# A state-space and mixture-of-experts layer on one core: the last scan direction and the last batch by token halves

## The chip, the core and the metric

The kernel runs on one core of a Trainium2 chip. The core has five instruction queues that run side by side and in order, each by itself: PE (TensorE, matrix products and transposes), DVE (VectorE), ACT (ScalarE), POOL (GpSimd) and SP (SyncE, which only issues transfers here). They wait for one another through semaphores. The metric is the device time of one execution in microseconds; less is better.

## The reference, cut to what matters

The input x has 8 batches of 1024 tokens and 256 features, all in float32. A batch goes through two blocks, each `x + layernorm(block(layernorm(x)))`.

```python
def _mamba_block(x, ...):                  # ED = 512 channels, N = 16 states
    xz = x @ W_in.T
    y = _ssm_branch(xf, zf, ...)           # tokens in order
    y_b = _ssm_branch(xb, zb, ...)         # tokens reversed, other weights
    return ((y + y_b[:, ::-1, :]) * 0.5) @ W_out.T

def _ssm_branch(...):
    x = silu(causal_depthwise_conv(xz_half)); delta = softplus(...)
    # for each token: h = exp(delta * A) * h + delta * B * x ;  y = sum over the states of h * C
    return (y + Dp * x) * silu(z)

def _L0_ffn_ref(hidden, ...):              # 8 experts, the best 2 of each token, and a shared one
    ...
```

The second block sends each token to its two best experts of eight (256 to 512 to 256) and adds a shared expert that all tokens go through.

## The kernel before, in words

**Scans.** A batch has two directions, so there are 16 windows w; the odd ones scan the tokens backwards. In a window there are 16 states n times 4 channel blocks c of 128 channels: 64 units, 1024 in all. Unit k needs on ACT one exponential, `feed_decay` (decay, 128 x 1024, in PSUM, two buffers), on POOL one product, `feed_drive` (xu times a row of B broadcast over the partitions, three buffers), and on DVE one `tensor_tensor_scan` over 1024 tokens, `scan_unit`. After the four units of a state the result h is turned to token-major by PE in 8 tiles of 128 tokens (`turn_tile`), and each tile is multiplied by its column of C and added to y (128 x 512): by DVE for three tiles of four (`sum_tile`), by ACT and POOL for the fourth (`scale_tile`, `pool_tile`; tiles 2, 6, 10 and 14 of 16). The rows of B come by `b_row_load`, one of 1024 tokens for each state, into two buffers. SP issues it as soon as the four drives of the state two before are made.

**Everything else is side work**, written out by hand as a list of pieces in `side_work`: the tokens' norm, the input projection (`proj`), the four taps of the convolution (`tap0` on ACT, `tap` on DVE), delta (`dt_mm`, `softplus`, `delta`), `u_mul` on POOL that turns xu into delta times x, and for a batch whose two windows are done the mixing: `y_dump` and `y_load` of y through DRAM, `z_mm`, `y_turn`, `y_add`, `gate`, `out_mm`, then norm, residual and norm (`ln_stats`, `ln_var`, `ln_rstd`, `ln_apply`, `res_add`), `xn2_turn`, the router, the routing on DVE (`peak`, `top1`, `top2`, `slots`; `owner_hot` is its last result), the `scatter` of the tokens to their experts' blocks by indirect DMA, the shared expert (`h1_mm`, `gelu`, `eo_mm`), the routed experts in six groups of four blocks (`xs_load`, `xs_turn`, `r1_mm`, `rgelu`, `r2_mm`, `ys_store`), the `gather` of their results, and the combine (`comb_mm`, `comb`), the last norm, `fin_add` and `out_store`.

**The order.** Time is cut into slots. Scan unit k stands in slot 2k on DVE, its drive in slot 2k-4 on POOL, its decay in slot 2k-3 on ACT; tile i is turned in slot i+7 and added in slot i+8 (POOL's in i+9). The table `AT` gives each piece of side work a due time, and `due // 16` is its slot (`Plan.put`). An engine goes through the slots and issues what stands in each. So `AT` fixes the order on each engine, and the semaphores fix the time. `BANK_USE` orders the uses of two PSUM banks by the side work in the same way. Window w starts at slot 128 w; the last, w = 15, at 1920, and the last scan stands in slot 2046. From b = 2 on, the batches in the middle have the same places, 256 slots apart.

**The end.** Batch 6's experts run beside window 15; its `gather` stands in slots 2061 to 2071. Batch 7 is mixed whole after that: first `y_turn` in slot 2087, last `out_mm` in 2117, `slots` in 2143, the first `xs_turn` in 2171, the first `gather` in 2262, the last `fin_add` in 2282.

`DMA_RING_BYTES` is given to the program as the size of the scratch for the descriptors that POOL makes for its indirect DMAs.

## Time and profile before

| | |
|---|---|
| median of 3 runs (lowest, highest) | 4735.8 us (4734.28, 4736.21) |
| the profiled execution | 4736.2 us |
| its span | 4735.0 us, 52683 instructions |
| PE busy | 3366.6 us (71%) |
| DVE busy | 3978.3 us (84%) |
| ACT busy | 2975.1 us (63%) |
| POOL busy | 3570.4 us (75%) |
| scan, L1104 | 1024 x 2.278 us |
| drive, L1567 | 1024 x 2.361 us |
| moved by DMA | 687.42 MB, 145 GB/s |

A line of a view names the line of the kernel, the engine, the operation and the tiles. "Idle before" is the time for which the engine stood still just before an instruction, with the releaser, the work that ended last among what it waited for; "issue" is idle time in which the profile shows nothing that it waited for. The execution's time is 1.2 us more than its span; that part lies outside what the trace shows.

### The profile page before, as it was taken

The page shows a single profiled execution, that of the slowest core. Times are in us where ns is not written, and L with a number is a line of the kernel's source. Part 1 is how long each engine was busy: PE and PEld are TensorE (multiplying, and loading weights), DVE is VectorE, ACT ScalarE, POOL GpSimd, SP SyncE. Part 2 cuts the span into 40 slices and gives each one's busy share as a digit, 9 for nine tenths or more (in the row PEclk, how much of TensorE's full clock was granted, in tenths as well). Part 3 has the DMA queues.
Part 4 walks back from the last instruction along what each step waited for, and adds up shares of the span by engine and source line. Part 5 has one row for each costly group of instructions (what it writes and reads, how often), then busy time and mean ns, then how long its engine had stood idle before and what let it go on. Part 6 is the DMA issues. An engine that isn't in the chain of part 4 may idle for free.

```text
span 4735.0 us, 52683 instructions
## 1 busy us (share of the span) xinstructions
PE 3366.6 (71%) x16720; PEld 2441.2 (52%) x16720; DVE 3978.3 (84%) x4136; ACT 2975.1 (63%) x4196; POOL 3570.4 (75%) x2119
## 2 busy tenths in 40 slices
PE   3466767786678857787778867777677866787575
PEld 1344445564456645565446644566446554476354
DVE  2899999898989989898989989898898989898200
ACT  4455756686657856686657856577566866576343
POOL 2698877978878878878879778887879788797111
PEclk8566777998779968898879977899779987798787
DMA  4321332555335642466325553356325553255244
GB/s 120 117 82 64 114 106 95 174 191 181 126 102 186 214 151 93 142 202 206 125 76 194 193 169 125 114 188 224 133 83 165 189 196 134 98 184 175 66 161 149
DMA packets 362017, 687.42 MB, mean 145 GB/s; under 512 B 31874, under 2 KB 205451, under 8 KB 357643
## 3 DMA queue, kind: packets, MB, share of 16 engines
q1 hardware_dynamic: 349450, 650.48, 41.5%
q0 software_dynamic: 12288, 33.57, 2.2%
q8 instruction: 133, 2.18, 0.2%
q14 instruction: 146, 1.19, 0.1%
HBM read 513.04 MB, written 170.92 MB: 144 GB/s over the span
## 4 chain that ended last, share of the span: by engine, by line
DVE 36%; POOL 21%; issue 21%; ACT 9%; PE 8%; DMA 4%; SPq 0%; DVEq 0%; POOLq 0%; ACTq 0%
DVE h L1104 17%; POOL drive L1567 12%; DVE y L1119 10%; DVE side L1182 3%; POOL y L1575 3%; POOL xs_dram L1620 2%; POOL work L1631 2%; ACT decay L1311 2%; DVE stats L1163 1%; POOL xu L1589 1%; PE h_t L947 1%; PE side L1082 1%; ACT work L1525 1%; ACT scaled L1329 1%; ACT work L1519 1%
## 5 line engine op out<-in xcount | busy, mean ns | idle before, releaser
L1567 POOL TENSOR_TENSOR drive<-xu,b_row 128x1024 f32<-128x1024 f32 x1024 | 2408.4, 2361 | 354.1 <-DVE h L1104 350.6
L1104 DVE TENSOR_TENSOR_SCAN h<-decay,drive 128x1024 f32<-128x1024 f32 x1024 | 2332.4, 2278 | 148.1 <-POOL drive L1567 121.7
L947 PE MATMUL h_t<-ident,h 128*128 128x128 f32 x8192 | 1472.0, 318 | 852.2 <-DVE y L1119 544.6
L947 PEld LDWEIGHTS h_t<-ident,h 128*128 128x128 f32 x8192 | 1092.6, 162 | 1355.9 <-DVE y L1119 807.3
L1311 ACT ACTIVATE decay<-delta,neg_a 128x1024 f32<-128x1024 f32 x1024 | 1142.7, 1117 | 874.5 <-DVE h L1104 841.2
L1119 DVE SCALAR_TENSOR_TENSOR y<-h_t,c_col,y 128x512 f32<-128x512 f32 x1488 | 1065.1, 732 | 65.6 <-PE h_t L947 64.1
L1575 POOL TENSOR_TENSOR y<-y,scaled 128x512 f32<-128x512 f32 x496 | 630.6, 1271 | 185.6 <-ACT scaled L1329 182.9
L1082 PE MATMUL side<-expert_w,work 128*128 128x256 f32 x1472 | 400.8, 424 | 69.1 <-issue 34.6
L1074 PE MATMUL side<-xn_t,expert_w 128*128 128x128 f32 x2944 | 388.5, 277 | 38.9 <-DVE xu L1182 14.8
L1329 ACT ACTIVATE scaled<-h_t,c_col 128x512 f32<-128x512 f32 x496 | 340.4, 686 | 115.0 <-PE h_t L947 113.8
L1074 PEld LDWEIGHTS side<-xn_t,expert_w 128*128 128x128 f32 x2944 | 355.0, 192 | 50.7 <-DVE xu L1182 17.7
L1082 PEld LDWEIGHTS side<-expert_w,work 128*128 128x128 f32 x1472 | 300.2, 213 | 128.1 <-issue 44.0
L1631 POOL DMA_INDIRECT work<-ys_dram,slot_i x128 | 123.6, 966 | 245.6 <-DMA ys_dram<-work 215.0
L1589 POOL TENSOR_TENSOR xu<-xu,prep_work 128x1024 f32<-128x1024 f32 x64 | 150.8, 2357 | 150.7 <-DVE prep_work L1149 150.7
L1182 DVE SCALAR_TENSOR_TENSOR side<-prep_work,chan_sb,side 128x512 f32<-128x512 f32 x256 | 191.9, 750 | 78.9 <-ACT side L1358 74.3
L1281 DVE TENSOR_TENSOR acc<-side,acc 128x512 f32<-128x512 f32 x32 | 21.7, 677 | 252.5 <-PE side L1059 244.1
L1519 ACT ACTIVATE work<-side,b_blocks 128x128 f32<-128x128 f32 x736 | 207.4, 365 | 40.2 <-PE side L1074 40.2
L1620 POOL DMA_INDIRECT xs_dram<-work,slot_i x128 | 126.3, 987 | 114.3 <-DVE owner_hot L1275 68.6
L985 PE MATMUL side<-dbc,wdt_sb 97*128 97x512 f32 x256 | 161.2, 734 | 13.2 <-DVE prep_work L1149 5.9
L965 PE MATMUL side<-xn_t,w_in_sb 128*128 128x512 f32 x256 | 136.4, 662 | 40.8 <-DVE xu L1182 30.4
L1059 PE MATMUL side<-work 128*128 128x256 f32 x256 | 104.8, 551 | 70.6 <-DMA work<-ys_dram,slot_i 54.1
L1003 PE MATMUL side<-w_out_sb,work 128*128 128x256 f32 x512 | 137.4, 419 | 21.8 <-POOL work L1611 14.5
(148 smaller groups left out, 3735.7 us busy)
## 6 DMA issues: line engine op xcount, KB each, us to landing
expert_w<-in_w SPq DMA_DIRECT2D x384, 512.0 KB, 4.2
b_row<-b_dram SPq DMA_DIRECT2D x256, 512.0 KB, 4.1
dx_dram<-prep_work SPq DMA_DIRECT2D x64, 512.0 KB, 3.7
delta_dram<-prep_work SPq DMA_DIRECT2D x64, 512.0 KB
delta<-delta_dram SPq DMA_DIRECT2D x64, 512.0 KB, 4.2
work<-xs_dram SPq DMA_DIRECT2D x40, 512.0 KB, 4.0
ys_dram<-work SPq DMA_DIRECT2D x40, 512.0 KB, 6.0
xz_dram<-prep_work SPq DMA_DIRECT2D x32, 512.0 KB, 2.7
```

Of the source, the lines that this page charges most:

```text
L947: t = pe.e.transpose(h_t[i % N_H_T][:, c * P:(c + 1) * P], h[:, gn % 2, c, tb * P:(tb + 1) * P], ident[:, :])
L1074: mm = pe.e.matmul(bank[:, m * P:(m + 1) * P], wi[:, k, m * P:(m + 1) * P], xn2_t[:, k, at:at + P], start=(k == 0), stop=(k == DC - 1))
L1082: mm = pe.e.matmul(bank[:, q % 2 * D:(q % 2 + 1) * D], h1_blocks[:, q, m, :], wo[:, m, :], start=(m == 0), stop=(m == HC - 1))
L1104: dve.e.tensor_tensor_scan(o, a, v, 0.0, ALU.mult, ALU.add).then_inc(scanned, 1)
L1119: dve.e.scalar_tensor_tensor(out=y[:, tb, :], in0=h_t[i % N_H_T][:, :], scalar=c_n, in1=y[:, tb, :], op0=ALU.mult, op1=ALU.add).then_inc(s ...
L1182: op = dve.e.scalar_tensor_tensor(out=into, in0=xz_pad[:, at:at + BANK], scalar=chan_col(d, c, CHAN_CONV_W + k), in1=bank[:, :], op0=ALU.m ...
L1311: act.e.activation(decay[k % N_DECAY][:, :], delta[:, c, :], ACT.Exp, scale=neg_a[:, c, w % 2, n:n + 1]).then_inc(decay_made, 1)
L1329: act.e.mul(into, h_t[i % N_H_T][:, :], c_col[:, w % 2, tb, n:n + 1]).then_inc(tile_scaled, 1)
L1519: op = act.e.activation(h1_blocks[:, q, m, :], side[bank_of["r1_mm", index]][:, m * P:(m + 1) * P], ACT.Identity, bias=b1_blocks[:, m, j:j ...
L1567: pool.e.tensor_tensor(drive[:, k % N_DRIVE, :], xu[:, w % 2, c, :], b_row[:, gn % N_B_ROW, :], ALU.mult).then_inc(drive_made, 1)
L1575: pool.e.tensor_tensor(y[:, tb, :], y[:, tb, :], scaled[:, at % N_SCALED, :], ALU.add).then_inc(gathered, 1)
L1620: pool.e.indirect_dma_start(out=xs_dram, out_offset=bass.IndirectOffsetOnAxis(ap=slot_i[:, r, tb:tb + 1], axis=0), in_=tokens[:, tb, :], i ...
```

## The change

1. The last window (`SPLIT` = 15) is scanned by halves of 512 tokens: first tokens 512 to 1023 for all 16 states, then tokens 0 to 511. A unit is now two channel blocks times 512 tokens, so there are still 64 units; each has two scans and two exponentials and one drive product of the same size. The state at the border is kept by ACT (`keep_h`, 16 copies of 128 x 4) and is the start of the second half's scans. The rows of B are loaded by halves: 32 loads of 512 tokens in the place of 16 of 1024. Tiles go to engines by the same rule.
2. The last batch is mixed by halves. Its first half is the one that the scan finishes first. Its `z_mm` and `z_silu` are done for both halves in window 15 (slots 1923 to 1993), `y_turn` to `out_mm` for the first half in 2004 to 2034, with the first norm's statistics and the residual up to 2043. y is turned from where it lies: `y_dump` and `y_load` fall away for this batch. z, the tokens and one of two buffers of the experts' inner results are put where `xu` of the even window lay, the sums in `prep_work`, the shared expert's inner result in a part of y. Norm, residual, norm, `x1_store`, the last norm and `out_store` are by halves.
3. For all batches: the bias product of `eo_mm` moves to `comb_mm`; `diag` moves from `work` to `xn2_t` (so `xn2_copy` waits for the combine of the batch before); x1 has two places in DRAM; `xn2_turn` and `xn2_copy` go by token half first, and `h1_mm` waits for its half alone; `top1` waits for the `mix_turn` of the batch before.
4. `DMA_RING_BYTES` is 2048 in the place of 1024.
5. All places in `AT` and `BANK_USE` are new. For the batches 3 to 7, counted from slot 256 b: `delta` of the even window's last block is due in slot 0 (before 5), the first `xz_load` in 1 (before 5), the first two `tap` in 5 and 8 (before both 5), the last `ys_store` of batch b-2, whose experts end here, in 16 (before 5), its `gather` in 18 to 27 (before 4 to 16). `u_mul` of the odd window's last block, for b = 5 say, in slot 103 (before 128). At the end: `gather` of batch 6 in slots 2042, 2043, 2043 and 2060 to 2069, `y_turn` of the second half 2069 to 2076, last `out_mm` 2087, `slots` 2107, first `xs_turn` 2136, first `gather` 2227, last `fin_add` 2248. `rank_mm` stands ahead of `mix_turn`.

```diff
-DMA_RING_BYTES = 1024
+DMA_RING_BYTES = 2048
...
+        def scan_halves(k):
+            hs, part, n, _ = half_state(k)
+            dve.wait_ge(decay_made, k + 1)
+            dve.wait_ge(drive_made, k + 1)
...
+                dve.wait_ge(turned, SPLIT * TILES + (hs - 3) * QB)
+                dve.wait_ge(h_kept, min(hs - 3, N))
+            if part:
+                dve.wait_ge(h_kept, n + 1)
+            for r in range(NH):
+                c = k % (EC // NH) * NH + r
+                its = slice(r * BANK, (r + 1) * BANK)
+                op = dve.e.tensor_tensor_scan(h_half(hs)[:, c, ::-1], decay[k % N_DECAY][:, its][:, ::-1],
+                                              drive[:, k % N_DRIVE, its][:, ::-1],
+                                              carried_h[:, n, c:c + 1] if part else 0.0, ALU.mult, ALU.add)
+            op.then_inc(scanned, 1)
...
+        def feed_halves(k):
+            hs, part, n, t = half_state(k)
+            act.wait_ge(scanned, k - N_DECAY + 1)
+            for r in range(NH):
+                c = k % (EC // NH) * NH + r
+                act.wait_ge(delta_in[c], 16 * (SPLIT + 1))
+                op = act.e.activation(decay[k % N_DECAY][:, r * BANK:(r + 1) * BANK], delta[:, c, t:t + BANK],
+                                      ACT.Exp, scale=neg_a[:, c, SPLIT % 2, n:n + 1])
+            op.then_inc(decay_made, 1)
+
+        def keep_h(i):
+            act.wait_ge(scanned, WHOLE + (i + 1) * (EC // NH))
+            act.e.copy(carried_h[:, i, :], h_half(i)[:, :, 0]).then_inc(h_kept, 1)
...
+                hs, part, n, t = half_state(k)
+                c = k % (EC // NH) * NH
+                pool.wait_ge(done["u_mul"], nth("u_mul", SPLIT, c + NH - 1))
+                op = pool.e.tensor_tensor(
+                    drive[:, k % N_DRIVE, :].rearrange("p (r t) -> p r t", r=NH),
+                    xu[:, SPLIT % 2, c:c + NH, t:t + BANK],
+                    b_row[:, row % N_B_ROW, 0:BANK].rearrange("p (a t) -> p a t", a=1).to_broadcast([P, NH, BANK]),
+                    ALU.mult)
...
+                    if row >= N_B_ROW:
+                        sp.wait_ge(drive_made, row_end(row - N_B_ROW))
+                    sp.e.dma_start(b_row[:, buf, 0:size], b_dram[w % 2, n:n + 1, cols].to_broadcast([P, size])
...
                 elif piece == "y_turn":
+                    if b < LAST:
+                        pe.wait_ge(done["y_load"], 16 * nth("y_load", b, s))
+                        its_y = y_half
+                    else:
+                        its_y = y[:, half_of(b, s) * QB:(half_of(b, s) + 1) * QB, :]
...
+                    o = bank[:, i % 2 * D:(i % 2 + 1) * D]
+                    pe.e.matmul(o, mix_t[:, tb * P:(tb + 1) * P], b2_sb[:, :], start=True, stop=False)
...
+                    elif b == LAST:
+                        sp.wait_ge(drive_made, WHOLE)
                     elif b:
                         sp.wait_ge(done["comb_mm"], nth("comb_mm", b - 1, TB - 1))
...
+                    else:
+                        sp.wait_ge(done["out_mm"], nth("out_mm", b, (s + 1) * QB - 1))
+                        t = half_of(b, s) * BANK
+                        for q in range(0, QB, 2):
+                            sp.e.dma_start(tokens_of(b, t // P + q, 2).rearrange("p (r d) -> p r d", d=D),
```

## Rows read from the trace of the kernel before

**Rows 1.** The page, busy tenths of DVE in 40 equal slices of the span.

```profile
DVE  2899999898989989898989989898898989898200
```

**Rows 2.** Busy time by stretch: a middle batch's length, last direction, tail; last columns PEclk, DMA share.

```profile
1280.00:1853.00 573.00, 423.94 (x2150) 307.82 (x2148) 522.80 (x554) 388.32 (x553) 466.09 (x272) 0.84 0.47 155
...
4143.00:4353.80 210.80, 175.25 (x1145) 147.76 (x1143) 203.45 (x161) 154.31 (x236) 189.20 (x97) 0.94 0.56 178
4353.80:4735.00 381.20, 240.10 (x1002) 175.88 (x1002) 47.11 (x141) 129.83 (x244) 67.39 (x74) 0.78 0.40 129
```

**Rows 3.** Groups by line: busy us, mean ns of one, idle before with its releasers.

```profile
L1567 POOL TENSOR_TENSOR drive<-xu,b_row 128x1024 f32<-128x1024 f32 x1024 | 2408.4, 2361 | 354.1 <-DVE h L1104 350.6
L1104 DVE TENSOR_TENSOR_SCAN h<-decay,drive 128x1024 f32<-128x1024 f32 x1024 | 2332.4, 2278 | 148.1 <-POOL drive L1567 121.7 <-ACT decay L1311 25.6
...
L1255 DVE TENSOR_TENSOR_SCAN sums<-carry,side 128x64 f32<-128x64 f32 x8 | 2.2, 275 | 3.7 <-PE side L1029 3.7
```

**Rows 4.** Timeline from last scan to batch 7's first y turn: start, length in us, engine, line.

```profile
4351.53 2.28 DVE L1104 TENSOR_TENSOR_SCAN h<-decay,drive 128x1024 f32<-128x1024 f32 x1
...
4360.68 1.26 POOL L1575 TENSOR_TENSOR y<-y,scaled 128x512 f32<-128x512 f32 x1 [1.66 <-ACT scaled L1329]
...
4380.94 0.95 POOL L1631 DMA_INDIRECT work<-ys_dram,slot_i  x1 [0.30 <-issue]
...
4398.43 0.37 SPq L1790 DMA_DIRECT2D work<-y_dram  x1
...
4404.85 3.72 PE L997 MATMUL side<-ident,work 128*128 128x128 f32 x16 [11.06 <-DMA work<-y_dram]
```

**Rows 5.** Timeline: second half's projection, first norm, turning, routing's first and last step.

```profile
4441.98 9.06 PE L1003 MATMUL side<-w_out_sb,work 128*128 128x256 f32 x32 [8.80 <-POOL work L1611]
...
4451.49 2.71 DVE L1163 BATCH_NORM_STATS2 stats<-acc 128x6 f32<-128x256 f32 x8 [11.00 <-ACT acc L1430]
...
4472.16 3.73 PE L1009 MATMUL side<-ident,work 128*128 128x128 f32 x16 [21.12 <-ACT work L1450]
...
4483.66 0.22 DVE L1212 TENSOR_TENSOR logits<-side,router_b_sb 128x64 f32<-128x64 f32 x1 [18.16 <-PE side L1016]
...
4498.09 0.23 DVE L1275 TENSOR_SCALAR owner_hot<-owner,lane 8x24 f32<-8x24 f32 x1
```

**Rows 6.** Timeline: scatter stall, routed rows' load, first routed product, last combine, store.

```profile
4509.38 0.95 POOL L1620 DMA_INDIRECT xs_dram<-work,slot_i  x1 [2.05 <-issue]
...
4524.56 0.37 SPq L1857 DMA_DIRECT2D work<-xs_dram  x1
...
4539.24 5.60 PE L1074 MATMUL side<-xn_t,expert_w 128*128 128x128 f32 x48 [0.99 <-ACT xn_t L1507]
...
4719.15 0.69 DVE L1281 TENSOR_TENSOR acc<-side,acc 128x512 f32<-128x512 f32 x1 [4.29 <-PE side L1059]
...
4730.52 0.38 SPq L1871 DMA_DIRECT2D out<-acc  x1
```

**Rows 7.** Timeline: four z products of batch 7's second half on PE.

```profile
4423.38 7.03 PE L991 MATMUL side<-xn_t,w_in_sb 128*128 128x512 f32 x16
```

**Rows 8.** What DVE waited for, 4150 to 4353 us: total us, times, longest.

```profile
DVE h L1104 <- ACT decay L1311: 4.2, 5, 0.8
DVE y L1119 <- PE h_t L947: 2.1, 1, 2.1
```

**Rows 9.** What DVE waited for, 3840 to 3900 us, the start of batch 7's first window.

```profile
DVE h L1104 <- POOL drive L1567: 7.1, 6, 1.3
DVE side L1182 <- ACT side L1358: 6.8, 1, 6.8
```

**Rows 10.** Timeline of POOL there: the first gather of batch 5's results.

```profile
3861.81 1.06 POOL L1631 DMA_INDIRECT work<-ys_dram,slot_i  x1 [5.72 <-DMA ys_dram<-work]
```

**Rows 11.** The page's DMA issues (median us to landing), and SP's waits: total, times, longest.

```profile
b_row<-b_dram SPq DMA_DIRECT2D x256, 512.0 KB, 4.1
...
SPq L1838 <- PE side L1082: 416.5, 154, 8.7
```

More of the change, by code:

```diff
@@ L710, in mamba_moe @@
     plan = Plan()
-    work = side_work(N, EC, NH, DC, HC, TB, QB, groups, loads)
+    work = side_work(NB, N, EC, NH, DC, HC, TB, QB, groups, loads)
     pieces = {piece: [index for b in range(NB) for index in indices(b)] for piece, (_, indices) in work.items()}
@@ L828, in mamba_moe @@
         N_FOUND = half // (TOP * D)
[L829 removed]
+        diag = xn2_t[:, 0, 0:2 * TOP * P].rearrange("p (k r t) -> p k r t", k=2, r=TOP)
+        carried_h = sb("carried_h", [P, N, EC])
         mix_t = work[0:NX, 2 * half:2 * half + L]
@@ L859, in mamba_moe @@
         scanned = sem("scanned")
+        h_kept = sem("h_kept")
+        own_res_in = [sem(f"own_res_in{s}") for s in range(NH)]
+        x1_out = [sem(f"x1_out{s}") for s in range(NH)]
         turned = sem("turned")
@@ new lines, in h1_blocks, with x1_of, part_tiles, row_of @@
+        def h1_blocks(b, G):
+            if b == LAST and G % 2:
+                return its_own[:, 0:half].rearrange("p (j m t) -> p j m t", j=GROUP, m=HC)
+            return h1_group
+        def x1_of(b):
+            return its_own[:, half:2 * half].rearrange("p (b d) -> p b d", b=TB) if b == LAST else x1_half
+        def part_tiles(b, s):
+            n = TB // norm_parts(b, NB, NH)
+            first = tile_of(b, s * n)
+            return first, n
+        def row_of(k):
+            return k // EC if k < WHOLE else SPLIT * N + (k - WHOLE) // (EC // NH)
@@ L903, in wait_y, with wait_tile @@
         def wait_y(engine, i):
-            before = i - TB
+            if i < SPLIT * TILES:
+                wait_tile(engine, i - TB)
+            elif state_of(i)[1] or i < SPLIT * TILES + QB:
+                wait_tile(engine, i - QB)
+            else:
+                wait_tile(engine, SPLIT * TILES - TB + state_of(i)[2])
+        def wait_tile(engine, before):
             if not by_pool(before):
@@ L1152, in side_piece @@
                     kind, at, j = index
-                    src, dst, (stats, mv, rstd, shift) = norm_io(kind, at)
+                    src, dst, first, n, (stats, mv, rstd, shift) = norm_io(kind, at)
                     if kind == "prep":
@@ L1165, in side_piece @@
                     kind, at = index
-                    src, dst, (stats, mv, rstd, shift) = norm_io(kind, at)
-                    n = src.shape[1]
-                    its_stats = "tok_stats" if kind == "prep" else "ln_stats"
+                    src, dst, first, n, (stats, mv, rstd, shift) = norm_io(kind, at)
+                    its_stats = norm_piece("stats", kind, at)
                     dve.wait_ge(done[its_stats], nth(its_stats, kind, at, n // 2 - 1))
-                    for tb in range(n):
+                    for tb in range(first, first + n):
                         op = dve.e.bn_aggr(mv[:, tb, :], stats[:, tb, :])
@@ L1437, in side_piece @@
+                    op = act.e.copy(xn2_of(b)[:, c, t:t + BANK], side[bank_of["xn2_turn", index]][:, :])
                 elif piece in ("tok_apply", "ln_apply"):
                     kind, at, j = index
-                    src, dst, (stats, mv, rstd, shift) = norm_io(kind, at)
-                    its_rstd = "tok_rstd" if kind == "prep" else "ln_rstd"
+                    src, dst, first, n, (stats, mv, rstd, shift) = norm_io(kind, at)
+                    its_rstd = norm_piece("rstd", kind, at)
@@ L1441, in side_piece @@
                     act.wait_ge(done[its_rstd], nth(its_rstd, kind, at))
                     if kind == "pre":
-                        act.wait_ge(done["res_add"], nth("res_add", at, TB // 2 - 1))
+                        act.wait_ge(done["res_add"], last_of_part("res_add", at))
                     if kind in ("post", "fin"):
                         into = free_bank(act, piece, index)[:, :].rearrange("p (r d) -> p r d", d=D)
+                    elif kind == "pre":
+                        into = tokens_of(at[0], first + 2 * j, 2).rearrange("p (r d) -> p r d", d=D)
@@ L1551, in act_program @@
                     feed_decay(k + N_DECAY)
+                hs, into = divmod(s - 2 * WHOLE - 5, 2 * EC // NH)
+                if not into and 0 <= hs < N:
+                    keep_h(hs)
                 i = s - 2 * EC
```

773 lines of the change are left out of this document (450 added, 323 removed), and 627 rows, old and new, of tables (AT, BANK_USE).

## The prediction

> **What bounds the kernel now.** I read the slices first: VectorE (DVE) is at 80 to 90% and more from the fifth to the 37th slice of 118 us, and near idle in the last three [rows 1]. So there are two stages. In the first, which ends with the last scan at 4353.8 us, DVE sets the pace: a batch in the middle takes 573 us with 522.8 us of DVE busy, and the last direction, 64 scan units in 210.8 us, has DVE at 203.5 us (97%), with POOL at 189.2 and PE at 175.3 [rows 2]. In the second, the tail of 381.2 us, no engine is full (PE 240.1, DVE 47.1) [rows 2]; it is one chain of dependent steps, and here latency counts. The timeline of the tail shows it [rows 4 to 6]. What the change is worth is the tail that it takes away, less what it puts under a DVE that is already full, plus what the new places do to seven batches.
>
> **The tail, step by step.** I count from E, the end of the last scan, 4351.53 + 2.28 = 4353.8 [rows 4]. Today the last y tile is done at E+8.1, the gathers of batch 6 end at E+28.1 (a gather issue costs 0.95 + 0.30 = 1.25 us), the load of y waits for batch 6's last add and goes out at E+44.6, the first y turn is at E+51.0 [rows 4], and the out-projection of the second half ends at E+97.2 [rows 5].
> With the change half 1 (tokens 512 to 1023) has been turned, gated and projected under the scans, z is there for both halves, and y is read where it lies. Three of the eight gather pairs stand before the last tiles. Left are 10 issues, 12.5 us, to E+21; POOL then makes one norm's rstd (2.4 us) and two gates of 1.3, to E+26; the next dx load follows the first gate (2.8 us, the median landing of that size), and with a second rstd between them the last two gates end at about E+35. PE's three shared-expert pieces ahead of the projection (1.8 us each) fit beside that, and the projection itself takes 9.1 [rows 5]: E+45. **52 us** are saved here.
> Norm, residual and second norm take 20.7 us for eight tiles [rows 5]. Of this 5 us are two rstd, which do not shrink; half of the other 15.7 is 7.9. I add 1.5, since ACT now has a copy of the shared expert ahead of the norm's apply and the residual load is issued late: 14.5, so E+60. Turning and router take 11.5 [rows 5]; the router stays whole, two of the four turns are gone: 9.3, E+69. Routing takes 14.7 to the end of owner_hot at 4498.3 [rows 5]; the rank product is now ahead of the transposes on PE, about 3 us less: E+81. **10.5 us** saved.
> From there to the first routed product it is 40.9 us today [rows 5, 6], because PE works at the shared expert until 4536.8. With half 1 of it done early, PE has one h1 piece and four eo pieces left (about 12 us), and the scatter becomes last: the load of its rows goes out 26.2 us after routing [rows 5, 6]; two stalls of 2.05 instead of 0.30 (one of them in [rows 6]) go if the larger ring does what it should, leaving 22.7; then 4 us of load and 2.4 of turn: 29. **12 us** saved, E+110.
> The routed part is the same list of pieces in the same order, and 195.8 us follow [rows 6]. The final norm now runs by halves; from the last combine to the store it is 11.4 us today [rows 6], of which half the statistics and applies, 4 us, go. E+302 against E+381.2. I put the gain at **78 us**. Bounds: 60 (each half's chain meets in-order queues, as the 1.5 above, and PE starts the routed groups after an idle of 10 us at the lower clock; its granted clock over the tail is 0.78 already [rows 2]) and 88.
>
> **What goes under the scans.** (a) 64 units of the last direction are two scans of 512 instead of one of 1024. 0.275 us for 64 columns and 2.278 for 1024 give 2.09 ns a column and 0.14 fixed [rows 3]; two of 512 are 2.42, with 0.03 between them: 64 x 0.17 = **+11 us**. Bounds 0 (no fixed part) and 64 x 0.275 = 18. The Trainium skill, "VectorE: DVE Perf Modes", section on the TRN2 errata, speaks against this edit: a fixed cost per instruction, so pieces of a tile pay it again, 120 cycles at 0.96 GHz where an input lies in PSUM. By that figure an estimate would be 64 x 0.125 = 8 us in place of the 11. The trace agrees in kind, with 0.14 us from two sizes.
> (b) DVE pieces of half 1 that stood in the tail: four y adds and two residual adds of 0.68, four statistics of 0.41 and their aggregates: **+6 us**, since DVE is at 97% there. Bounds 4 and 9.
> (c) PE gets eight z pieces (1.76 each [rows 7]), four y turns and four projections of 2.3: +26 on 175 us in a window that grows to 228: 88%. POOL gets four gates, a norm and six gather issues, +15 on 189: 90%. ACT gets 64 second exponentials (0.1 to 0.2 each) and 16 small copies on 154. None is above DVE's 220, but queues are in order, and the six routed groups of batch 6 are squeezed from about 20 slots each to 16 to 18. Today DVE waits only 6 us in this window [rows 8]. The rows of B are halved too, so each of two buffers is freed every second unit: a load of 4.1 us has 6.9 us where it had 13, and behind it on SP stand expert loads that wait up to 8.7 us for PE [rows 11]. The drives are made up to three units ahead, so most of this is hidden; **+8 us**, bounds 0 and 30.
> The 16 copies of the state on ACT are waited for four states later; I cost them at nothing, and 0.2 us each (3) if ACT were the bound.
>
> **The seven other batches.** Two things can be read. From batch 3 on, delta of the even window is due five slots earlier and the load of xz with it, so the first tap no longer meets its own load: 6.8 us of DVE idle each [rows 9], five times, 34. But the gathers of batch b-2, which fall there too, move to slots 18 to 27 of the window, eight in nine slots instead of twelve. POOL then has about 38 us of work against 28 of DVE, and still waits for the store before them (5.7 us today, beside the tap's wait [rows 10]), say 3. That is 13 of stall against today's 7.1 + 6.8 + 2 [rows 9]; about 3 net, five times, 15. I take **-12 us**, bounds -34 and +20, since all places move by some slots. The ring: a scatter stall of this kind comes about once in two batches beside the tail; **-3 us**, bounds -8 and 0. The bias product that moves from the shared expert into the combine, and the diagonal's new place, add nothing to DVE; I cost them at nothing while PE is busy for 423.9 us of a batch's 573 [rows 2].
>
> **Sum.** 4735.0 - 78 + 11 + 6 + 8 - 12 - 3 = 4667 us of span. The profiled run took 4736.2, 1.2 more than its span, and the median of the three runs is 0.4 below it: **4668 us**.
>
> **Rivals.** A, the tail only. The places' refit gives nothing or loses a little, and the halves under the scans cost the upper bounds: 4735 - 70 + 15 + 6 + 20 + 8 = 4714. For it: PE and POOL near 90% with DVE at 97%. Against: DVE waits little there today. 0.14.
> B, the gain of the refit is whole: -34 and -8, the tail 85, +17: 4735 - 85 + 17 + 3 - 42 = 4628. For it: the tap's stall is real; against: POOL takes its place. 0.10.
> C, slower: the half rows of B. Place: SP's queue in the last direction, where an expert load that waits for PE stands ahead of a row that POOL needs within 6.9 us. Price: each of the 32 rows late by x. The gain of 68 us is lost when x is above 68/32 = 2.1 us on average, and 2.4 us makes it slower by what can be told; at 3 us it gives 4668 + 96 = 4764. For it: waits of 8.7 us occur on SP; against: their mean is 416.5/154 = 2.7 [rows 11], and POOL runs ahead. 0.05.
> D, the change does not do what it says: half 1 is held until after the last scan (its dx loads, its gates behind the gathers), so only the reread of y and the order are won, 35 us: 4735 - 35 + 25 - 15 = 4710, inside A's time. 0.05.
> The main case, 0.66, by itself spans 4640 to 4700.
>
> **How the numbers follow.** A measurement of this kernel can tell about 0.2%, 9.5 us, from no change. Faster by more: the main case and B, and A and D but for 0.03 of them: 0.92. Within: 0.03. Slower: C, 0.05. The range has to leave out no more than 2 in 10: 4625 takes in B, 4716 takes in A and D.
>
> **What would show it.** In the profile after: the last scan ends at 4353.8 + 25 - 15, near 4364, and the end follows 302 us later; from the last scan to the first routed product 110 us, not 185; the scan of 512 columns 1.21 us; DVE idle in the last direction under 15 us; the 6.8 us before the tap gone from batches 3 to 7, with more idle for POOL's drive in its place; no 2.05 us before a scatter. Wrong I am if a b_row load or PE's turns hold the last direction (its 64 units over 245 us), if the middle batches leave 573 us by more than 5 either way, or if the tail's first steps wait in order for batch 6's gathers past E+50.

## The result: slower by 0.8%

| | before | after |
|---|---|---|
| median (lowest, highest), 5 runs each | 4735.8 us (4734.28, 4736.81) | 4771.64 us (4763.72, 4784.02) |
| ratio, with its 95% interval | 1 | 1.0079 (1.006 to 1.0099) |
| the profiled execution, its span | 4736.2, 4735.0 us | 4780.39, 4779.1 us |
| up to the start of window 2 | 586.9 us | 589.6 us |
| windows 2 to 13 | 3249.0 us | 3320.0 us |
| window 14 | 308.8 us | 298.3 us |
| the last direction, window 15 | 209.1 us | 256.0 us |
| from the last scan to the end | 381.2 us | 315.1 us |

I had forecast 4668 us and 4716 as the upper end. The lower part of the table is worked out from the starts of the scans in the two traces. It says where the time went: the stages before the last window lost 2.7 + 71.0 - 10.5 = 63.2 us, the last direction 46.9 us, and the tail gave back 66.1 us. Together that is +44 us, the difference of the two spans. The medians are 35.8 us apart: the profiled execution of the changed kernel took 8.8 us more than its median.

The page of the changed kernel, with the slices of DVE and of PE's granted clock and four groups; the columns are busy time, mean ns of one, and idle time before with its main releaser:

```profile
span 4779.1 us, 52822 instructions
PE 3469.0 (73%) x16720; PEld 2542.9 (53%) x16720; DVE 3977.1 (83%) x4200; ACT 2993.8 (63%) x4276; POOL 3574.2 (75%) x2131
...
DVE  2999998998989888888888888899888988988500
...
PEclk8566777997879887788778978789778987799887
...
L1254 DVE TENSOR_TENSOR_SCAN h<-decay,drive 128x1024 f32<-128x1024 f32 x960 | 2189.4, 2281 | 93.3 <-POOL drive L1787 59.5
L1085 PE MATMUL h_t<-ident,h 128*128 128x128 f32 x8192 | 1515.7, 325 | 803.8 <-DVE y L1287 538.1
...
L1287 DVE SCALAR_TENSOR_TENSOR y<-h_t,c_col,y 128x512 f32<-128x512 f32 x1488 | 1075.3, 737 | 196.1 <-PE h_t L1085 193.7
```

DVE's slices are at 8 or 9 tenths to the 37th as before (10 nines from the fifth on where [rows 1] had 18), and only two are near empty at the end where [rows 1] had three. The full stage is longer with the same busy time: DVE waits 193.7 us for PE's turned tiles in the whole run. By stretch (columns as in [rows 2]): windows 2 to 13, the last direction, the tail:

```profile
589.60:3909.60 3320.00, 2492.31 (x12393) 1844.23 (x12393) 2968.88 (x3078) 2201.75 (x3097) 2656.09 (x1529) 0.83 0.46 151
4208.00:4464.00 256.00, 205.59 (x1223) 169.89 (x1221) 217.52 (x238) 188.02 (x338) 203.90 (x114) 0.91 0.54 169
4464.00:4779.10 315.10, 220.86 (x944) 164.82 (x944) 41.39 (x126) 113.76 (x223) 63.44 (x78) 0.78 0.41 131
```

What DVE waited for in windows 2 to 13, first in the kernel before, then in the changed one; the columns are us in total, times, longest:

```profile
DVE h L1104 <- POOL drive L1567: 103.8, 60, 5.6
DVE y L1119 <- PE h_t L947: 52.6, 70, 2.0
DVE side L1182 <- ACT side L1358: 37.8, 6, 7.8
DVE h L1104 <- ACT decay L1311: 12.8, 19, 1.0
```

```profile
DVE y L1287 <- PE h_t L1085: 141.1, 134, 4.2
DVE h L1254 <- POOL drive L1787: 58.4, 22, 5.6
DVE prep_work L1360 <- DMA prep_work<-dx_dram: 31.0, 8, 7.7
DVE h L1254 <- ACT decay L1490: 23.1, 21, 3.5
DVE acc L1457 <- PE side L1207: 20.3, 13, 3.6
...
DVE side L1349 <- ACT side L1550: 14.2, 12, 6.0
DVE y L1284 <- PE h_t L1085: 8.7, 4, 3.5
```

The waits for POOL's drives fall by 45 us and those of the taps by 24. In their place come 92 us for tiles (141.1 + 8.7 against 57.8 with the first tiles of a window), 23 for the load of dx, 10 for decays and, among smaller ones, some 17 for the combine's product on PE (`acc`, L1457). The last is not a matter of the places: in the two kernels of the next section it is 13.9 us with the changed structure and the old places, and 1.8 us with the old structure and the new places. It goes with the structure, whose edit of the combine is the bias product that moved there.

A single late tile in the timeline of window 9 (start, length, engine, line, operation; in brackets the idle time before):

```profile
2585.65 1.91 ACT L1740 ACTIVATE work<-work 128x2048 f32<-128x2048 f32 x1
...
2587.58 1.28 ACT L1741 ACT_TABLE_LOAD   x1
...
2588.88 0.69 ACT L1521 ACTIVATE scaled<-h_t,c_col 128x512 f32<-128x512 f32 x1
...
2589.62 1.12 PE L1085 MATMUL h_t<-ident,h 128*128 128x128 f32 x4 [2.05 <-ACT scaled L1521]
...
2590.53 3.08 PE L1230 MATMUL side<-expert_w,work 128*128 128x256 f32 x8
...
2593.44 0.60 PE L1085 MATMUL h_t<-ident,h 128*128 128x128 f32 x4
2593.88 1.89 PE L1230 MATMUL side<-expert_w,work 128*128 128x256 f32 x8
2594.08 0.75 DVE L1287 SCALAR_TENSOR_TENSOR y<-h_t,c_col,y 128x512 f32<-128x512 f32 x1 [2.56 <-PE h_t L1085]
```

ACT is in a gelu of a routed group and frees a tile's bank late; PE stands for 2.05 us, then makes the tile, then an `r2_mm` piece in 3.08 us (PE is at the lower of its two clocks, 1.2 GHz: the granted clock is 0.50 from 2584.0 to 2590.5 us, and 1.00 from 2593.5; the next such piece takes 1.89), and only then the tile that DVE needs. Three things lie in this one wait of 2.56 us: ACT's long activation, the clock, and a piece of side work between two tiles in each of two neighbouring slots. The experiments take them up one by one.

### The profile page after: what moved, and what is told of

Same layout as the page of the kernel before. It is cut to its first block, busy times and chain, and to the rows that moved or that the text cites. A ratio compares the mean times of both kernels' runs of the same rounds, so it can differ in the third digit from the quotient of the medians.

```text
span 4779.1 us, 52822 instructions
## 1 busy us (share of the span) xinstructions
PE 3469.0 (73%) x16720; PEld 2542.9 (53%) x16720; DVE 3977.1 (83%) x4200; ACT 2993.8 (63%) x4276; POOL 3574.2 (75%) x2131
## 4 chain that ended last, share of the span: by engine, by line
DVE 28%; PE 20%; issue 16%; POOL 14%; ACT 11%; DMA 10%; SPq 1%; DVEq 0%; POOLq 0%; ACTq 0%
DVE h L1254 12%; POOL drive L1787 7%; DVE y L1287 7%; PE h_t L1085 4%; PE side L1230 4%; DVE side L1349 2%; DMA dx_dram<-prep_work 2%; POOL xs_dram L1851 2%; POOL y L1805 2%; PE side L1207 2%; ACT decay L1490 2%; PE side L1148 2%; DMA delta_dram<-prep_work 1%; DMA expert_w<-in_w 1%; PE side L1129 1%
## 5 line engine op out<-in xcount | busy, mean ns | idle before, releaser
L1254 DVE TENSOR_TENSOR_SCAN h<-decay,drive 128x1024 f32<-128x1024 f32 x960 | 2189.4, 2281 | 93.3 <-POOL drive L1787 59.5
L1085 PE MATMUL h_t<-ident,h 128*128 128x128 f32 x8192 | 1515.7, 325 | 803.8 <-DVE y L1287 538.1
L1085 PEld LDWEIGHTS h_t<-ident,h 128*128 128x128 f32 x8192 | 1143.9, 167 | 1294.8 <-DVE y L1287 779.6
L1490 ACT ACTIVATE decay<-delta,neg_a 128x1024 f32<-128x1024 f32 x960 | 1071.3, 1117 | 698.8 <-DVE h L1254 655.2
L1287 DVE SCALAR_TENSOR_TENSOR y<-h_t,c_col,y 128x512 f32<-128x512 f32 x1488 | 1075.3, 737 | 196.1 <-PE h_t L1085 193.7
L1222 PE MATMUL side<-xn_t,expert_w 128*128 128x128 f32 x2944 | 414.4, 290 | 62.7 <-DMA expert_w<-in_w 20.6
L1230 PE MATMUL side<-expert_w,work 128*128 128x256 f32 x1384 | 383.9, 429 | 56.1 <-issue 26.5
L1222 PEld LDWEIGHTS side<-xn_t,expert_w 128*128 128x128 f32 x2944 | 378.9, 203 | 80.7 <-ACT work L1733 22.3
L1733 ACT ACTIVATE work<-side,b_blocks 128x128 f32<-128x128 f32 x692 | 196.3, 369 | 46.7 <-PE side L1222 46.1
L1457 DVE TENSOR_TENSOR prep_work<-side,prep_work 128x512 f32<-128x512 f32 x4 | 2.8, 691 | 204.6 <-PE side L1207 204.6
L1851 POOL DMA_INDIRECT xs_dram<-work,slot_i x112 | 110.7, 988 | 76.2 <-DVE owner_hot L1450 47.2
L1109 PE MATMUL side<-xu,wx_sb 128*96 128x512 f32 x256 | 138.4, 673 | 25.8 <-ACT xn_t L1715 10.0
```

What stands on the lines that cost most here:

```text
L1085: t = pe.e.transpose(h_t[i % N_H_T][:, c * P:(c + 1) * P], its_h[:, c, :], ident[:, :])
L1222: mm = pe.e.matmul(bank[:, m * P:(m + 1) * P], wi[:, k, m * P:(m + 1) * P], xn2_t[:, k, at:at + P], start=(k == 0), stop=(k == DC - 1))
L1230: mm = pe.e.matmul(bank[:, q % 2 * D:(q % 2 + 1) * D], h1_blocks(b, G)[:, q, m, :], wo[:, m, :], start=(m == 0), stop=(m == HC - 1))
L1254: dve.e.tensor_tensor_scan(o, a, v, 0.0, ALU.mult, ALU.add).then_inc(scanned, 1)
L1287: dve.e.scalar_tensor_tensor(out=y[:, tb, :], in0=h_t[i % N_H_T][:, :], scalar=c_n, in1=y[:, tb, :], op0=ALU.mult, op1=ALU.add).then_inc(s ...
L1490: act.e.activation(decay[k % N_DECAY][:, :], delta[:, c, :], ACT.Exp, scale=neg_a[:, c, w % 2, n:n + 1]).then_inc(decay_made, 1)
```

## The experiments

### Where: the places ahead of window 14, put back and put in alone

In the first kernel every piece of side work that stood ahead of slot 1776 before stands there again (but for `share_diag`, whose tile lies elsewhere in the changed structure), and the two banks are used in that order; the rest is the changed kernel. The second is the opposite: the kernel before with the new places ahead of slot 1776. A few of its pieces beside slot 1776 had to be moved, since in the first form of it (`e4`), which gave no time, the engines wait for one another for good. The diff shows two lists, for batch 4 alone.

```diff
-    "rgelu": [..., 22928, 23264, 23601, 23920, 24368, 24737, ...],
+    "rgelu": [..., 22816, 23264, 23584, 23888, 24288, 24608, ...],
-    "out_mm": [..., 21424, 21440, 21456, 21472, 21744, 21760, 21776, 21792, ...],
+    "out_mm": [..., 21185, 21216, 21264, 21296, 21568, 21584, 21600, 21616, ...],
...
```

> The changed kernel in its structure (halves, bias product in the combine, diagonal in xn2_t, new waits, ring of 2048), but every piece of side work that the kernel before has ahead of slot 1776 (16 slots ahead of window 14) stands where it stood there, and the two PSUM banks are used in that order too. Theory P: the 74.5 us that window 14 starts late are gone but for a few, so 4771 - 70 = 4701 us, window 14 starts near 3840. Theory S (the structural edits that hold for all batches, such as xn2_copy that waits for the combine of the batch before and the bias product moved to the combine, cost the time): stays at 4771, window 14 starts near 3910.

> The kernel before in its structure, its last window scanned whole, its ring of 1024 and its places from slot 1776 on, but with the new places (and order of the two banks) for all side work ahead of slot 1776. With the old places back in the changed kernel window 14 started near where it did before, at 4696.9 us for the whole. Theory P (the new places alone lose the time): 4736 + 65 = 4801 us, window 14 starts near 3905, odd windows at a granted clock near 0.90 in the place of 0.98, DVE waits some 14 us in each for turned tiles. Theory PS (the places lose only together with the structural edits, for instance xn2_copy behind the combine of the batch before): 4736 to 4760 us.

Measured: with the old places back 4696.9 us, ratio 0.9915 (0.9899 to 0.9932), the last scan 81 us earlier than in the changed kernel. It beats both kernels. The new places alone: 4817.5 us, ratio 1.0175 (1.0159 to 1.0192). Windows 2 to 13 take 3250.3 and 3331.6 us. Their two first waits of DVE there, old places back and new places alone:

```profile
DVE h L1248 <- POOL drive L1781: 84.2, 56, 5.6
DVE y L1281 <- PE h_t L1079: 46.5, 63, 1.9
```

```profile
DVE y L1117 <- PE h_t L945: 166.7, 137, 5.9
DVE h L1102 <- POOL drive L1565: 65.7, 33, 5.6
```

So the places cost 75 us in the one structure and 83 in the other (4734.8 beside it). The structural edits that hold for all batches cost nothing that shows (3250.3 against 3249.0 us): they bring 11 us of waits for the combine's product (13.9 against 2.8), and the waits for drives are 20 us shorter (84.2 against 103.8). The halves and the tail, with the ring, are worth 39 us net.

### The ring

```diff
-DMA_RING_BYTES = 2048
+DMA_RING_BYTES = 1024
```

> The changed kernel with DMA_RING_BYTES back at 1024, nothing else. In the changed kernel the window 14 starts 74.5 us later than before (3910.3 against 3835.8). Theory P (the new places of the side work in windows 1 to 13 make DVE wait for PE's turned tiles): the ring has no part in it, 4771 us within 10, with at most two or three stalls of 2.05 us back before a scatter. Theory R (the larger ring is what slows the gathers and drives of POOL): 4700 us, the 74 us gone.

> The kernel before with DMA_RING_BYTES 2048, nothing else. Theory P: 4736 us or up to 5 less, since a stall of 2.05 us before a scatter comes about once in two batches. Theory R: 4800 us. The prediction's term was -3 us with bounds -8 and 0.

Measured: 4793.6 us (1.012, 1.0103 to 1.0137) with the small ring in the changed kernel, 4738.3 us (0.9998, 0.9989 to 1.0008) with the large ring in the kernel before. The stalls of about 2.05 us before a scatter go from nine to one there (18.8 us to 2.1, counted from 500 us on), and the time doesn't move: POOL's stall was hidden. In the changed kernel such stalls, here of 1.6 to 4.1 us, are nine with the small ring and three with the large one (15 us less), and the larger ring is worth some 20 us; theory P had allowed 10. The wait that passes them on is that for POOL's drives. In windows 2 to 13 with the small ring (3341.0 us for 3320.0) it is 20 us longer than the 58.4 above, and no other grows by more than 2 us:

```profile
DVE h L1254 <- POOL drive L1787: 78.6, 30, 5.6
```

### Is it PE's clock?

```diff
             def turn_tile(i):
+                if i + 2 * EC - 1 in FILL:
...
+                        pe.wait_ge(summed, summed_to(i - N_H_T))
+                    for c in range(4):
+                        pe.e.transpose(h_t[i % N_H_T][:, c * P:(c + 1) * P], ident[:, :], ident[:, :])
```

> The changed kernel with idle time of PE filled: in windows 1 to 15, in each slot in which no piece of side work stands on PE (some 700 slots), PE makes four transposes of the identity into the tile's PSUM bank before it waits for the scan; the tile's own four then overwrite them. It adds about 0.42 us to PE in such a slot and no information. Theory C (PE falls to the lower of its two clocks after it stood idle, and the pieces that come next then take twice as long and hold back the tiles): the granted clock in window 11 rises from 0.90 to 0.97 or more, DVE's wait for tiles there falls from 13.8 us to under 8, and the time falls by 25 us or more, to 4745 or less. Theory O (the order of the pieces ahead of the tiles holds them back at any clock, or PE has too much work): no gain or a loss of up to 40 us, 4770 to 4810.

> The changed kernel with the old places ahead of slot 1776 (4696.9 us) plus the same filling of PE's empty slots. Its odd windows run at a granted clock of 0.98 already, its even ones at 0.77 to 0.80 and its last at 0.9. Theory C: 5 to 25 us less, from the last window and the even ones, 4672 to 4692. Theory O: 4697 to 4730.

Measured: 4763.9 us (1.0055, 1.0038 to 1.0072), 8 less than the changed kernel, and 4690.5 us (0.9911, 0.9895 to 0.9928) with the old places, 6 less than without. Both intervals overlap those of the kernels without the fill, so neither gain is clear of noise. Windows 2 to 13 of the filled changed kernel, by stretch and by DVE's wait for tiles:

```profile
591.80:3908.30 3316.50, 2590.04 (x14716) 2016.71 (x14715) 2971.82 (x3078) 2206.92 (x3098) 2659.36 (x1529) 0.90 0.46 151
```

```profile
DVE y L1296 <- PE h_t L1094: 146.6, 136, 3.5
```

The granted clock rose from 0.83 to 0.90 and the waits for tiles stayed. In window 11, for which theory C had asked 0.97 and under 8 us, it is 0.94 with 15.9 us of waits for tiles. Theory C fell there; with the old places 4690.5 us lies inside its range. The fill can't stand where PE itself waits for the bank, as in the timeline above, so this test is weak for just those waits; the next pairs decide.

### Is it ACT's long activations against the scaled tiles?

ACT scales a tile in the slots that are 2 modulo 4. The first kernel moves the changed kernel's activations behind such tiles, the second moves those of the kernel before one slot ahead of them (batch 4's shown).

```diff
-    "rgelu": [..., 22928, 23264, 23601, 23920, 24368, 24737, ...],
+    "rgelu": [..., 22944, 23264, 23601, 23919, 24367, 24737, ...],
```

```diff
-    "rgelu": [..., 22816, 23264, 23584, 23888, 24288, 24608, ...],
+    "rgelu": [..., 22815, 23263, 23583, 23888, 24287, 24607, ...],
```

> The changed kernel with only the places of 33 of ACT's long activations moved (18 rgelu, gelu and z_silu pieces ahead of slot 1792, the rest behind), nearly all by one slot, into the slots that are 2 modulo 4. In these slots ACT scales its tile of y first, and the next tile to scale comes four slots (some 4.6 us) later; such an activation with its two table loads takes 4.5 us. In the kernel before 30 of 36 rgelu of batches 1 to 6 stand so, in the changed one 17. PE stands idle for 1.5 us or more ahead of a tile until ACT has scaled, 18 times (49.1 us) in windows 2 to 13 of the changed kernel, 6 times (20.6 us) in those before; its next piece of side work then runs at the lower clock (3.1 to 3.7 us for 1.9) and DVE waits for the tile behind it. Theory A (this phase against the scaled tiles is the main cause): such idle falls to 8 times or fewer, DVE's waits for tiles in windows 2 to 13 fall from 149.8 us to under 110, and the time falls by 20 us or more, to 4750 or less. Theory B (bursts of pieces on PE between two tiles are the main cause, two 1.9 us products in neighbouring slots of 1.17 us): less than 10 us are won, 4762 to 4772, and the waits for tiles stay above 130 us.

> The kernel before with 35 of its rgelu issued one slot earlier on ACT (from the slots that are 2 modulo 4 into those that are 1 modulo 4, behind all the r1 copies that they need); nothing that follows them is moved. By due time alone nothing gets later. Theory A (an activation of 4.5 us right ahead of a tile that ACT must scale holds PE and DVE): each of the 35 delays a tile by some 2 to 3 us, of which DVE's two h_t buffers and the scan hide about 1: slower by 20 to 60 us, 4756 to 4796, with 30 or more idle times of PE of 1.5 us and more for the scaled tile. Theory B: unchanged, 4730 to 4742.

> The kernel of the changed structure with the old places ahead of slot 1776 and PE's empty slots filled (4690.5 us), with 29 long activations of ACT moved to the slots that are 2 modulo 4, ten of them in the last two windows. Theory A: 8 to 20 us less than 4690, most of it in the last direction (247.2 us there), so 4670 to 4682. Theory B: 4686 to 4694.

Measured: 4798.7 us (1.0132, 1.0105 to 1.0158); of the 33 places 23 lie ahead of slot 1792, not 18 as I wrote, and the slot of 1.17 us in that text is wrong too: in the odd windows of the kernel before it is 1.84 us (235.2 / 128), so that a scaled tile comes each 7.3 us, not each 4.6. 4802.8 us (1.0132, 1.0113 to 1.0152) for the kernel before with its gelus one slot earlier. 4726.9 us (0.9972, 0.9961 to 0.9983) for the mix, 36 more than without the moves, where the theories had forecast 4694 at most. PE's waits from 586 to 3885 us, the kernel before and then the one with the gelus one slot earlier:

```profile
PE h_t L947 <- DVE y L1119: 363.9, 306, 3.7
PE h_t L947 <- DVE h L1104: 139.8, 76, 11.2
PE h_t L947 <- ACT scaled L1329: 53.8, 62, 3.7
```

```profile
PE h_t L944 <- DVE y L1116: 343.5, 273, 3.7
PE h_t L944 <- ACT scaled L1326: 154.6, 70, 5.0
PE h_t L944 <- DVE h L1101: 121.1, 66, 10.4
```

The mechanism exists and is strong: 35 activations issued one slot earlier, nothing later, cost 67 us (I had put 20 to 60), and PE's long idle times for a scaled tile (1.5 us or more) go from 6 to 31. But it isn't what the change lost by: in the changed kernel these idle times fell from 18 to 9 as forecast, and the waits for tiles stayed (155.3 us), while the waits for decays rose from 23.1 to 41.9. Theory A fell. Its rival was right that the tiles stay late, not that the time stays: the moved activations now hold the decays.

### PE's load or ACT's: the same places with half of each taken away

```diff
                 elif piece == "r2_mm":
...
-                    for m in range(HC):
+                    for m in range(HC // 2):
...
                 elif piece == "rgelu":
-                    op = act.e.activation(its, its, ACT.Gelu)
-                    act.e.preload_act_table_set("natural_log_exp_and_others")
+                    op = act.e.activation(its, its, ACT.Identity)
```

The first edit stands for all of PE's heavy pieces, the second for the three kinds of activation; each is in kernels of its own.

> The changed kernel with about half of the products of PE's heavy side pieces left out, in all batches: of proj, z_mm, h1_mm and r1_mm one of two channel halves, of out_mm, eo_mm and r2_mm two of four products. To be read against the same edit on the kernel with the old places ahead of slot 1776; without the edit the two are 74.8 us apart (4771.6 and 4696.9), of it 69.7 in windows 2 to 13 (3320.0 and 3250.3 us). Theory P1 (PE's load, in bursts by the new places, holds the tiles): with half the load the two kernels come within 25 us. Theory P2 (PE is only held by ACT, whose long activations stand badly): they stay 50 us or more apart.

> The changed kernel with the old places ahead of slot 1776, and the same half of PE's products left out. Theory P1: 4660 to 4690 us, within 25 us of the one with the new places. Theory P2: the two stay 50 us or more apart.

> The changed kernel with the gelu of the shared and the routed experts and the silu of z left out (copied through ACT instead, 1.9 us with no table load around them, where they took 4.5 us). To be read against the same edit on the kernel with the old places ahead of slot 1776. Theory P2 (the long activations hold tiles and decays in the new places): the gap of 74.8 us falls to 25 us or less. Theory P1: the gap stays 50 us or more.

> The changed kernel with the old places ahead of slot 1776, and the same three activations replaced by copies. Theory P2: within 25 us of the one with the new places. Theory P1: 50 us or more below it.

| | new places | old places back | gap | gap in windows 2 to 13 |
|---|---|---|---|---|
| whole | 4771.6 | 4696.9 | 74.8 | 69.7 |
| PE's side products halved | 4652.0 | 4630.6 | 21.4 | 19.1 |
| ACT's long activations as copies | 4706.1 | 4633.4 | 72.7 | 59.7 |

Each of these kernels leaves a part of the work out, and only the differences of their times count. The gap closes with PE's load and not with ACT's. (The kernel with the old places came out 30 us below the 4660 to 4690 that I had written for it.) Windows 2 to 13 with the new places and PE's products halved, by stretch and by wait:

```profile
580.20:3828.40 3248.20, 2184.67 (x10116) 1565.29 (x10115) 2965.76 (x3079) 2196.16 (x3098) 2653.59 (x1530) 0.78 0.47 154
```

```profile
DVE y L1287 <- PE h_t L1085: 75.5, 74, 3.5
```

and the wait with the old places and the products halved:

```profile
DVE y L1281 <- PE h_t L1079: 39.0, 52, 1.4
```

The waits for tiles halve with the new places and hardly change with the old ones, and that at a lower granted clock (0.78 for 0.83). So PE's side work, with its full length and in the new places, is what holds the tiles. The work is the same in both orders; its places differ. Worked out from the trace of windows 2 to 13, by the piece on PE directly ahead of each tile that DVE waited for by 0.3 us or more: an `r2_mm` piece stands there 22 times (31.7 us) where it stood 5 times (3.0), an `out_mm` piece 13 times (17.6 us) where it stood once (0.5). With the products halved the two stand there 16 times (14.2 us). They make up 46 of the 92 us; the rest is spread over nearly all other kinds (`dbc_mm`, `z_mm`, `h1_mm`, `eo_mm`, `proj`, `r1_mm`, 7 to 10 us more each).

What it is in the new places that does it, the runs don't show. The four out-projections of batch 4's first half now stand in four neighbouring slots (1339 to 1342), before in 1324, 1326, 1329 and 1331. Each takes 1.89 us at the full clock, and 3.6 to 3.75 at the lower, and with the tile's 0.6 that is 2.5 and more in a slot of 2.4 us (310.9 us for the 128 slots of an even window). But those of the second half stood in four neighbouring slots before too (1348 to 1351, now 1359 to 1362), and 8 of the 13 waits are behind second halves, whose four stood in neighbouring slots before in every batch. Nor does a count over the tables tell the two orders apart: of the slots of windows 2 to 13, 413 have a long product (`proj`, `z_mm`, `out_mm`, `h1_mm`, `eo_mm`, `r1_mm`, `r2_mm`) with another in the next slot in the new order, and 433 in the old one; two or more in one slot stand in 29 and in 17. The lower clock has a part that stays open: of the 35 `r2_mm` and `out_mm` pieces above, 15 took 2.6 to 3.75 us, with 27.5 us of waits behind them, and 20 took 1.7 to 2.2 us, with 21.8. No run puts one kind of piece back alone. ACT's activations as copies gain some 65 us in either kernel; that they cost is true, but it is no part of the difference.

### The load of dx

```diff
-    "out_store": [..., 25297, ...],
+    "out_store": [..., 25457, ...],
```

> The changed kernel with the out_store of batches 0 to 6 issued 10 slots later (slot 1591 in the place of 1581 for batch 4), nothing else. DVE waits four times 4.6 to 7.8 us (36.6 us with the smaller ones, 9.4 us before) in the middle of the even windows for the load of dx from DRAM, which waits on SP for the store of dx ahead of it; that store was issued 0.8 us behind the 1 MB of out_store and 1.2 us behind the load of y (1 MB) and took over 8 us to land. Theory D (the store queues behind these 2 MB): the waits for dx fall under 20 us and the time by 8 to 20 us, to 4752 to 4764. Rival (the wait is given back by the next wait of the same window, for instance of POOL's drive): the waits for dx fall but the time stays within 5 us of 4771.

Measured: 4780.5 us (1.008, 1.0055 to 1.0105). The waits for dx in windows 2 to 13 fell from 31.0 to 17.7 us, so the store of dx did queue behind the output; but the time did not fall, and delta's wait for ACT rose from 14.7 to 23.5 us. The rival, "given back", was right in kind; its 5 us around 4771 were too narrow (the interval overlaps that of the changed kernel).

### The last direction

```diff
-                        for k in range(DC):
+                        for k in range(1 if b == LAST - 1 else DC):
```

> The changed kernel with the old places ahead of slot 1776 (4696.9 us, its last direction 251.7 us with 25.7 us of DVE waiting for PE's tiles), and of batch 6's first expert product only the first half of the channels is multiplied (the other half is left out): 56 pieces with four products in the place of eight, some 25 us less of PE beside the last window. Theory L (PE's load beside the last window makes DVE wait): DVE's wait for tiles falls under 12 us and the last direction is 238 us or less, the whole 4684 or less. Theory H (the time of the last direction is DVE's own, two scans per unit and the half batch's pieces, and the waits come from the order): 249 us or more, the whole 4694 or more.

Measured: 4692.0 us (0.9909, 0.9892 to 0.9925), the last direction 245.4 us with 19.5 us of waits for tiles. Neither theory's number: 16 us less of PE gave 6 us. The later pairs add to it. With PE's products halved the direction takes 242.4 us (old places) with 14.6 us of waits for tiles, with ACT's activations as copies 238.2 us with 14.4. PE and ACT both hold it, and neither alone.

## Why the prediction was wrong, point by point

**The tail: right in kind, -66 for -78.** The stations, counted from the end of the last scan at 4464.0 as forecast and as measured: last tile +8, +14; gathers of batch 6 +21, +26; second out-projection +45, +57; second norm +60, +71; router +69, +80; routing +81, +94; first routed product +110, +124; end +302, +315. The first three steps lost 12 us, and each of the next ones is as forecast within 2 us. (By its own stations the forecast is 381 - 302 = 79; its middle part adds up to 11.4 and not 10.5.) Here is where:

```profile
4460.98 1.05 POOL L1863 DMA_INDIRECT work<-ys_dram,slot_i  x1 [5.44 <-DMA ys_dram<-work]
...
4465.14 2.08 PE L1207 MATMUL side<-work,xn_t 128*128 128x256 f32 x4 [6.45 <-DMA work<-ys_dram,slot_i]
...
4468.96 0.75 DVE L1287 SCALAR_TENSOR_TENSOR y<-h_t,c_col,y 128x512 f32<-128x512 f32 x1 [4.98 <-PE h_t L1085]
...
4511.92 3.32 PEld L1148 LDWEIGHTS side<-w_out_sb,xu 128*128 128x128 f32 x16 [2.24 <-ACT y L1674]
...
4578.07 0.96 POOL L1851 DMA_INDIRECT xs_dram<-xu,slot_i  x1 [2.12 <-issue]
```

The gathers that were moved ahead of the last tiles wait for batch 6's last store, PE's combine waits for them and the last tiles wait behind that combine. I had moved the gathers and not asked what PE has queued behind them. The shared expert's copies on ACT stood ahead of the projection; I let them "fit beside". One stall of 2.12 us is left with the large ring (the prediction wanted none).

**(a) two scans per unit: 7 us for 11.** The scan of 512 took 1.207 us, and 1.267 where it starts from the kept state (forecast 1.21). Two of one unit overlap by some 0.08, so the scans of the last window are busy 153.0 us against 145.8. My fixed part of 0.14 us a scan was right (2 x 1.207 - 2.278 = 0.136 us); what I had wrong is the overlap, where I had put 0.03 between the two. The estimate of 8 from the fixed cost in the Trainium skill, "VectorE: DVE Perf Modes", section on the TRN2 errata, was nearer than mine; the trace agrees with it in size (0.125 us a scan against 0.136). That the total of 7.2 us is so near to 8 is luck in part, since the overlap and the 0.06 for the kept state, which it leaves out, go against each other.

```profile
L1270 DVE TENSOR_TENSOR_SCAN h<-decay,carried_h,drive 128x512 f32<-128x512 f32 x64 | 78.4, 1267 | 0.3 <-ACT decay L1499 0.3
L1270 DVE TENSOR_TENSOR_SCAN h<-decay,drive 128x512 f32<-128x512 f32 x64 | 74.6, 1207 | 10.3 <-POOL drive L1793 9.0 <-ACT decay L1499 1.1
L1287 DVE SCALAR_TENSOR_TENSOR y<-h_t,c_col,y 128x512 f32<-128x512 f32 x96 | 68.9, 738 | 29.2 <-PE h_t L1085 28.9
```

**(b) DVE's moved pieces: 6 us, as forecast** (2.7 + 1.4 + 1.3 + 0.4).

**(c) the queues: +33 for +8, past the bound of 30.** DVE's idle time in the last direction is 39 us for 6, and 28.9 of it are waits for PE's tiles. I had written that none of the engines was above DVE's 220 us, and for that took the smallest part of a range. PE at 206 us of 256 and ACT at 188 were below DVE and held it all the same, as the runs on the last direction show.

**The middle: +63 for -12, and beyond the bound of +20. This is the step that failed.** The term of -12 us for the seven other batches was made of two stalls, that of the taps and that of POOL, and left all other moved places at nothing. The taps' stall fell by 24 us (I had put 34). POOL's I had the wrong way round: where I expected more waits for its drives there were 45 us less. What the term had left out, PE's side work in its new places ahead of the tiles that DVE adds, cost 92 us of waits, and the loss in time is 75 us (4771.6 against 4696.9 with the old places). I had the lists of both orders before me and compared due times of the pieces that waited, not what now stood on PE ahead of the tiles. My bounds came from the pieces that I had looked at, with one sentence for "all places move by some slots". The two edits that I did cost at nothing, the bias product in the combine and the new place of the diagonal, cost nothing in time (3250.3 against 3249.0 us), though the combine now makes DVE wait 11 us more. The reason that I gave for them, a PE that is busy for 74% of a stretch, was none: 75% (2492 of 3320 us) did not keep the new places from holding DVE.

**The ring: -3 forecast; nothing in the kernel before**, and about 20 us in the changed one, as the pair of runs shows. They lie in the middle stage: without them its +63 would be some +84.

**The rivals.** C (the half rows of B) didn't happen: POOL has no wait for a row of B in the last direction. D didn't either; half 1 was done under the scans. B's gain of the refit was there in part (24 of the 34 us of the taps) and was overpaid. The case that came, slower by a refit that trades POOL's waits for PE's, I didn't have; A's refit that "loses a little" is the nearest, at 4714 us.

**The signs that I named** did their work: middle batches longer by more than 5 us, the last direction over 245, the tail's first steps past +50. But the 573 us of [rows 2] that I called a middle batch is a stretch somewhat longer than one. From the scans' starts two windows take 546 us before (2195.4 to 2741.6) and 557 to 565 after.

## What to carry to other kernels

An order table is not priced by the pieces whose stall it removes, nor by busy shares. Ask of every engine what now stands ahead of each deadline of the critical loop; how to count that from the table alone, these runs don't show. When a change has a structural part and a refit of places, run each alone: here the structure with the old places was worth 0.85% and the refit lost 1.6 to 1.75%. Three attempts to move a wait by hand gave it back elsewhere or lost more.

## What I had not expected of the hardware

An activation of 4.5 us with its two table loads, issued one slot (some 1.84 us) earlier in 35 places, cost 67 us, 1.9 us each, while no engine was full but DVE. A scan that starts from a column in SBUF takes 0.06 us more than one that starts from zero (1.267 against 1.207 us at 512 columns), and two scans in a row overlap by 0.08 in the records. A larger scratch for indirect DMAs took eight of nine stalls of 2.05 us away without moving the time of one kernel, and was worth 20 us in another, where DVE waited that much less for POOL's drives.
